# Attention's last steps in a post-norm transformer block: projection and turning of x1 cut into pieces, the count of the weights' rests moved ahead

## The reference

```python
q, k, v = (proj(w, b) for w, b in ((wq, bq), (wk, bk), (wv, bv)))      # 16 heads of 8
attn = softmax(einsum("bhqd,bhkd->bhqk", q, k) / sqrt(16))
out = einsum("bhqk,bhkd->bhqd", attn, v)
x = layernorm(x + out @ wo.T + bo)                                    # called x1 below
h = silu((x @ w1.T) * w1_s) * ((x @ w2.T) * w2_s)                      # 512 wide
h = gelu((h @ h1.T) * h1_s)
h = gelu((h @ h2.T) * h2_s)
x = layernorm(x + (h @ w3.T) * w3_s)
```

## Time and profile before

| | us |
|---|---|
| median of 3 runs | 448.09 |
| lowest and highest | 446.45, 448.43 |
| the profiled execution | 446.64 |
| its span, first to last instruction | 444.8 |
| TensorE, matmuls busy | 429.2 (96%) |
| VectorE busy | 385.5 (87%) |
| ScalarE busy | 368.1 (83%) |
| GpSimd busy | 90.5 (20%) |

### The profile page before, as it was taken

The page is one execution under the profiler, slowest core; times in us unless marked ns, Lnnn a source line. Parts: engine busy times, 40 slices in busy tenths (PEclk is TensorE's granted clock), DMA queues, the critical chain, the costliest instruction groups (busy, mean ns, idle before and its releaser), DMA issues.

```text
span 444.8 us, 9805 instructions
## 1 busy us (share of the span) xinstructions
PE 429.2 (96%) x3484; PEld 225.6 (51%) x3486; DVE 385.5 (87%) x724; ACT 368.1 (83%) x696; POOL 90.5 (20%) x142
## 2 busy tenths in 40 slices
PE   8999999999999999999999999999899899999993
PEld 3544444444444444444444443545343488877882
DVE  5589999999999999999999999999739477657636
ACT  4477888989998899998899899999889976678762
POOL 9810000100000010000001002372310262046103
PEclk9999999999999999999999999999999999999997
DMA  5665840110130111013011111121021000000101
GB/s 148 181 204 104 291 146 28 49 28 27 49 122 25 34 42 28 27 47 122 25 42 36 25 27 49 15 41 55 9 39 48 13 8 1 1 3 1 47 1 47
DMA packets 16988, 24.88 MB, mean 56 GB/s; under 512 B 5040, under 2 KB 8880, under 8 KB 16560
## 3 DMA queue, kind: packets, MB, share of 16 engines
q1 hardware_dynamic: 16304, 23.62, 19.1%
q10 hardware_dynamic: 640, 0.66, 0.6%
HBM read 15.08 MB, written 7.60 MB: 51 GB/s over the span
## 4 chain that ended last, share of the span: by engine, by line
PE 77%; DVE 12%; ACT 7%; issue 2%; POOL 0%; POOLq 0%; DVEq 0%; ACTq 0%
PE ps L1306 24%; PE ps L1228 21%; PE ps L1402 15%; DVE negmax L940 9%; PE ps L1290 9%; ACT arena L634 4%; PE ps L1170 2%; PE ps L1181 2%; DVE arena L930 1%; PE ps L1247 1%; PE ps L1352 1%; PE ps L1201 1%; PE ps L1256 1%; ACT v_pad L692 1%; ACT arena L647 1%
## 5 line engine op out<-in xcount | busy, mean ns | idle before, releaser
L940 DVE TENSOR_REDUCE negmax<-ps 128x1 f32<-128x512 f32 x458 | 275.3, 683 | 0.4 <-PE ps L1228 0.4
L634 ACT ACTIVATE arena<-ps 128x512 f32<-128x512 f32 x360 | 189.5, 611 | 19.9 <-PE ps L1290 15.1
L1290 PE MATMUL ps<-qx,kx 64*128 64x512 f32 x512 | 172.7, 453 | 1.2 <-DVE negmax L940 0.9
L1228 PE MATMUL ps<-kx,qx 61*128 61x512 f32 x464 | 160.1, 444 | 0.8 <-ACT arena L655 0.6
L1228 PEld LDWEIGHTS ps<-kx,qx 61*128 61x128 f32 x464 | 74.4, 184 | 91.2 <-DVE negmax L940 83.5
L1306 PE MATMUL ps<-arena,v_pad 128*32 128x256 f32 (+3 forms) x1328 | 104.6, 407 | 3.1 <-ACT arena L634 3.0
L634 ACT ACTIVATE hf<-ps 128x512 f32<-128x512 f32 x152 | 83.1, 603 | 8.2 <-PE ps L1290 7.0
L1290 PEld LDWEIGHTS ps<-qx,kx 64*128 64x128 f32 x512 | 80.0, 184 | 14.0 <-ACT arena L634 7.4
L1402 PE MATMUL ps<-hid,w_high 128*128 128x512 f32 (+1 forms) x296 | 68.2, 387 | 0.8 <-issue 0.4
L1402 PEld LDWEIGHTS ps<-hid,w_high 128*128 128x128 f32 x296 | 54.2, 188 | 12.4 <-issue 0.8
L1306 PEld LDWEIGHTS ps<-arena,v_pad 128*32 128x32 f32 x1328 | 28.4, 108 | 39.2 <-issue 31.2
(11 more groups left out here) (96 smaller groups left out, 322.6 us busy)
## 6 DMA issues: line engine op xcount, KB each, us to landing
qx<-parts_q SPq DMA_DIRECT2D x60, 64.0 KB, 2.1
late_sb<-in_late SPq DMA_DIRECT2D x3, 1280.0 KB, 5.6
kx<-parts_k SPq DMA_DIRECT2D x48, 64.0 KB, 2.1
parts_q<-prt SPq DMA_DIRECT2D x3, 512.0 KB, 5.2
parts_q<-arena SPq DMA_DIRECT2D x3, 512.0 KB, 5.7
xT_sb<-in_xT SPq DMA_DIRECT2D x4, 256.0 KB, 4.0
kx<-parts_k SPq DMA_DIRECT2D x8, 128.0 KB, 3.3
xT_sb<-arena SPq DMA_DIRECT2D x28, 32.0 KB
```

The costliest lines, as they stand in the source:

```text
L634: nc.scalar.activation(probs(n // HG)[:, heads(n), :], ps[:, PLAN["score", n][0], :], ACT.Exp, scale=SCALE).then_inc(exp_done, 1)
L940: nc.vector.tensor_reduce(negmax[:, t // TURNS % 2, m % 2, h * QT + q:h * QT + q + 1], ps[:, MAX_BANK + m % 4, :], AX.X, ALU.max, negate=T ...
L1228: nc.tensor.matmul(ps[:, MAX_BANK + m % 4, :], qx[at, slot, qc, h, q * P:(q + 1) * P], kx[at, slot, h, part * C:(part + 1) * C], start=Tru ...
L1290: nc.tensor.matmul(ps[:, bank, :], kx[at, slot, h % PAIR, kt * P:(kt + 1) * P], qx[at, slot, qc, h % PAIR, :], start=True, stop=True)\
```

## The change

In the table `BEHIND`, the output projections of chunks 0 and 1, four tiles each behind steps 117 and 118, are put one tile a step behind steps 114 to 121. The turnings of x1, four tiles each behind steps 121 and 122, are put two tiles a step, chunk 0 behind steps 122 and 123, chunk 1 behind 125 and 126. The count of the rests goes from behind step 125 to behind step 124, and waits for both operations of the first split. On VectorE all comparisons and folds of the rests stand ahead of the first statistics, behind a new wait for step 113; chunk 0 is taken from its statistics to its split before the statistics of chunk 1; the split of chunk 1 comes behind the flag `inexact`. The second gate tile gets a wait for that split.

```diff
+HF_STEPS = max(k for k in range(TAIL) if k % 3 == 2) + 1
@@ VectorE
             norm(0)
             norm(1)
-            first_stats(0)
-            first_stats(1)
-            invert(1)
-            first_apply(0)
-            first_apply(1)
+            dve.wait_ge(pv_done, HF_STEPS)
             flag(0, FLAGGED, 0, 1)
             fold(4, 2)
-            split_x1(0)
-            split_x1(1)
             fold(2, 3)
             fold(1, 4)
             flag(FLAGGED, SLICES, 1, 5)
             fold(2, 6)
             fold(1, 7)
+            invert(1)
+            first_stats(0)
+            first_apply(0)
+            split_x1(0)
+            first_stats(1)
+            first_apply(1)
             dve.wait_ge(counted, 1)
...
             nc.vector.tensor_scalar(inexact[:], any_more[:], 0.0, None, ALU.is_gt).then_inc(inexact_set, 1)
+            split_x1(1)
             invert(2)
@@ TensorE
-            def out_proj(c):
+            def out_proj(c, t0=0, t1=TILES):
...
-            def turn_x1(c):
+            def turn_x1(c, t0=0, t1=TILES):
...
             def count():
 
                 pe.wait_ge(flagged, FOLDS)
-                pe.wait_ge(x1_split, 1)
+                pe.wait_ge(x1_split, 2)
...
-            BEHIND = {STEPS - 11: (out_proj, 0), STEPS - 10: (out_proj, 1),
-                      STEPS - 7: (turn_x1, 0), STEPS - 6: (turn_x1, 1), STEPS - 3: (count,)}
+            BEHIND = {STEPS - 14 + t: (out_proj, t // TILES, t % TILES, t % TILES + 1) for t in range(2 * TILES)}
+            BEHIND.update({STEPS - 6: (turn_x1, 0, 0, 2), STEPS - 5: (turn_x1, 0, 2, TILES), STEPS - 4: (count,),
+                           STEPS - 3: (turn_x1, 1, 0, 2), STEPS - 2: (turn_x1, 1, 2, TILES)})
@@ TensorE, gate_tile
                 if m == 0:
                     pe.wait_ge(x1_split, 2 * c + 2)
+                if n == 1:
+                    pe.wait_ge(x1_split, 4)
```

More of the change, by code:

```diff
@@ L1337, in _ @@
             pe.wait_ge(over, WHOLE - FOLD)
-            def out_proj(c):
-                pe.wait_ge(chunk_normed, c + 1)
-                if c == 0:
+            def out_proj(c, t0=0, t1=TILES):
+                if t0 == 0:
+                    pe.wait_ge(chunk_normed, c + 1)
+                if c == 0 and t0 == 0:
                     pe.wait_ge(in_mid, 32)
@@ L1349, in out_proj @@
                     pe.wait_ge(gated, MT + 2)
-                for t in range(TILES):
+                for t in range(t0, t1):
                     at = slice(c * C + t * P, c * C + (t + 1) * P)
@@ L1353, in out_proj @@
                                            start=True, stop=True)
-                ins.then_inc(wo_done, 1)
-            def turn_x1(c):
-                pe.wait_ge(x1_ready, c + 1)
-                for t in range(TILES):
+                if t1 == TILES:
+                    ins.then_inc(wo_done, 1)
+            def turn_x1(c, t0=0, t1=TILES):
+                if t0 == 0:
+                    pe.wait_ge(x1_ready, c + 1)
+                for t in range(t0, t1):
                     ins = nc.tensor.transpose(ps[:, X1T_BANK[c], t * P:(t + 1) * P],
                                               x1[:, c * TILES + t, :], ident[:])
-                ins.then_inc(x1_turned, 1)
+                if t1 == TILES:
+                    ins.then_inc(x1_turned, 1)
             def count():
                 pe.wait_ge(flagged, FOLDS)
-                pe.wait_ge(x1_split, 1)
+                pe.wait_ge(x1_split, 2)
                 nc.tensor.matmul(ps[0:1, INEXACT_BANK, :], ones[:], nonzero[:, 0, :],
                                  start=True, stop=True).then_inc(counted, 1)
-            BEHIND = {STEPS - 11: (out_proj, 0), STEPS - 10: (out_proj, 1),
-                      STEPS - 7: (turn_x1, 0), STEPS - 6: (turn_x1, 1), STEPS - 3: (count,)}
+            BEHIND = {STEPS - 14 + t: (out_proj, t // TILES, t % TILES, t % TILES + 1) for t in range(2 * TILES)}
+            BEHIND.update({STEPS - 6: (turn_x1, 0, 0, 2), STEPS - 5: (turn_x1, 0, 2, TILES), STEPS - 4: (count,),
+                           STEPS - 3: (turn_x1, 1, 0, 2), STEPS - 2: (turn_x1, 1, 2, TILES)})
             for g in range(-RUN_BEFORE, GROUPS_ALL):
```

## The result

| | kernel before | kernel after |
|---|---|---|
| median, us | 447.75 (4 runs, 446.45 to 448.43) | 451.45 (4 runs, 450.40 to 451.84) |
| profiled execution, us | 446.64 | 450.40 |
| its span, us | 444.8 | 448.6 |
| mean granted clock | 0.995 | 0.990 |

The ratio is 1.0089, 95% interval 1.0066 to 1.0112. Forecast was 448.7 in a range of 446.1 to 450.6: the time lies outside. The forecast was a change of +0.6 us, on the median of the three runs that there were then (448.09 us); measured are +3.7 us, on 447.75.

What follows compares the result with a forecast made beforehand. ScalarE's exponentials, 1.96 us a step, set attention's pace. Net +0.45 us at the last product (2.0 won, 2.5 given back), +0.1 queue, +0.05 tight steps: +0.6 on 448.09, so 448.7 us, range 446.1 to 450.6.

Steps and rivals of the forecast that it cites:

- The new wait: TensorE waits 2.4 us at the turning of chunk 1 for VectorE; last product +0.45 us net.
- P(125): Start of the products of attention step 125; the turning of chunk 1 behind it would be reached at 343.49.
- rival A: TensorE doesn't wait at the turning of chunk 1; the full 2.0 us are kept, 446.1 us; chance 0.12.
- The projection, one tile a step: Eight 0.27 us insertions behind P(114) to P(121): first costs 0.17 us, others 0 to 0.03; lump losses 0.82 and 0.79 go.
- the free 0.28 us: TensorE's spare time in each attention step, within which an insertion would not delay ScalarE's exponentials.
- The half turnings: x1 turned two tiles a step, 0.30 us each, costing 0 to 0.03; the lumps' 0.30 and 0.29 us go.
- S(127): Start of the first exponential of attention step 127: forecast 346.77 where 344.30 was due, 2.47 us lost.
- Rival C: Clock falls in the new pause; the gate's first 16 matmuls take 4.09 us more, 452.8 us; chance 0.08.
- Rival B: SyncE's queue decides: late last gathers hold up VectorE's gate products, 0.5 to 1.0 us beyond forecast, 449.4; chance 0.13.
- The part of the flags: Comparisons and folds ahead of the first statistics fill VectorE's idle 7.59 us: worth 0, from 0 to +0.1 us.

Runs made afterwards that it cites:

- the kernel put right: Kernel after with VectorE's two calls exchanged, reciprocal early, turnings of chunk 1 behind steps 124 and 125, count behind 126: 446.43 us, ratio 0.9976 to the kernel before.

## Why the prediction was wrong

**The new wait: right, in place and size.** The step said that TensorE waits 2.4 us behind P(125), from VectorE's order; it waited 2.38, and ScalarE 2.43 before the last four exponentials (2.47 forecast). Exchanging the order took it away. VectorE's idle 7.59 us were filled as foreseen, but it now idled 8.05 us in front of the first split, with the statistics of chunk 1 waiting behind that split. So rival A, no wait and the full 2.0 us, did not come.

**The projection, one tile a step: the size was wrong, and with it the first term of the sum.** The step divided the lump's 1.09 us by four. A group has a fixed part: singles, pairs and lumps alike fit 0.20 us and 0.22 us a tile for the projection. The cause of the fixed part was not tested; the trace has the first weight load of a group start together with its first matmul (both at 321.24), so no weights are loaded during the products in front of it. With 0.42 us TensorE needs 0.99 + 0.66 + 0.42 = 2.07 us a step, against ScalarE's 1.96, and becomes the bound: P(115) at 322.32, P(116) at 324.40 (the next single tile stands 2.08 us behind the one before). I had called the free 0.28 us an edge and then taken 0 to 0.03 a step; it was 0.11. The half turnings were sized the same way, 0.30 us, and took 0.37. S(127) came at 347.66 instead of 346.77. Of the 2.0 us that the lumps had cost, half were lost at once.

**Rival C came true, beside the forecast, not in its place.** I had given it 0.08, since the trace of before had 1.00 over waits of up to 0.9 us, and priced it at 4.1 us with the drop over the gate. The drop lasted from 347 to 351, over the steps 126 and 127, where part of it lay under ScalarE's exponentials; in the profile it puts off the last products by about 0.7 us and lengthens them by 0.2, and filling the pause gave back 1.6 us by the ratios (0.35%, of which a part is the gather's, for TensorE's wait in the gate was 0.34 us, against 1.26 and 0.82). All three profiles that have the pause (the two of the kernel after, and the one with the early reciprocal) have the drop right behind it, and none of the others has one there. The mean clock of all runs of the kernel after is below 0.994. The Trainium skill's "TensorE: Matmul & The Clock Gate", "Part 4: PE-mode transpose", would have the transposes not count in the way that other matmuls do. The runs with the exchanged order and with dummies have the same transposes without the pause, at 1.00; none has the pause without the transposes, so whether they had a part in it is still open. The section "HAM oscillation — how this bites in real kernels" of the same page warns of pauses of TensorE. The run with dummies agrees in kind; the page speaks of longer pauses than the 2.4 us that were enough here, and where the two differ the measurement decides.

**Rival B came true as well.** The step took 0.1 us from 0 to 0.8; TensorE waited 1.26. Two of its numbers failed. The second split came 2.3 us later than I had it (350.58 for 348.3): 1.1 us by the products of step 126 (347.99 for 346.90), the rest by these products and the transposes behind them at half clock. And the last gather landed 3.1 us behind its issue, not 1.7. The kernel before had a cover of 1.9 us (last gather issued at 352.3 and landed at 354.0, reciprocal at 355.89), which the late split and store had just used up: with 1.7 us the gather would have landed at 358.4, 0.2 us after VectorE had come free. The other 1.4 us of its wait are the slower landing. In all four profiles in which the gathers follow 0.7 us behind the load (both of the kernel after, the exchanged order, the dummies) their median landing is 1.9 to 2.4 us and VectorE waits, 0.70 to 1.63. In the other nine, with 1.5 us or more between them, the median is 1.7, though in three of them one gather takes 3.1 to 3.7, and VectorE doesn't wait. So the 1.7 us were taken from one execution, and from an order of the queue that the change took away. That the load is what holds the gathers up was not tested. The reciprocal put early gave back 1.3 us by the ratios (0.3%) and 1.0 to 1.5 by the tail times.

**The failure of the working is that B and C were weighed as other outcomes.** Both hang on the same late turning that the forecast itself named, so they had to be added to it: 0.45 + 0.9 for the tiles + 0.9 for the clock + 1.1 to 1.5 for the gather is 3.4 to 3.8, and 3.7 was measured. How deep the clock would fall, and that it would at all, the rows of the kernel before could not tell.

The part of the flags was rightly put at 0, as its run alone shows.

## What to carry to other kernels

When a change puts one engine's work behind a wait of another, write down what each later wait had to spare, and take the new delay through all of them: the delays add up, and a slack of 1.9 us further down was used up by them. A time read from one order of a queue, like the 1.7 us of the gathers, need not hold in another. Cutting a lump into pieces pays a fixed part for every piece; take it from a row with few tiles, not from the lump's mean, and compare it with the slack of a step. And look at the order of the engine that feeds the pieces: here two exchanged calls on VectorE turned a loss of 0.8% into 0.2%, and with the early reciprocal and the table in the same order the change became a gain of 0.2%.

## What the hardware showed

A pause of TensorE of 2.4 us, with full steps in front of it, was followed by 1.2 GHz from about 347.5 to 350.9 us (from the clock of the three stretches), while TensorE was at work again; so it was in all three profiles with the pause. With nine dummy matmuls in the pause the clock stayed at 2.4 GHz.

Behind waits of 0.94 and 0.67 us close to each other the clock fell to 1.2 GHz in two of eleven profiles. By the tail times such a drop cost about 1.4 us in the kernel put right (41.49 against 40.12 without it).

A small group of fp32 matmuls (128 x 128 by 128) between products and scores took 0.20 us and 0.22 us a tile (one tile 0.42, two 0.65, four 1.09).

Four small DMAs (2 KB each) issued one behind the other by the same queue landed 1.7 us after their issue, in the kernel before, and 1.7 to 3.1 us in the kernel after, where they followed 0.7 us behind a load of 64 KB.
